# A graph-attention kernel: the message product reads its weights from PSUM, VectorE copies them, and the logits have three PSUM banks for four

## The reference

```python
xl = (x @ W_l).reshape(n, H, C)          # n = 6250, H = 4 heads, C = 64
xr = (x @ W_r).reshape(n, H, C)
feat = xl[src] + xr[dst]
feat = jnp.where(feat >= 0, feat, NEG_SLOPE * feat)
logits = jnp.einsum('ehc,hc->eh', feat, att)
seg_max = jax.ops.segment_max(logits, dst, num_segments=n)
ex = jnp.exp(logits - seg_max[dst])
seg_sum = jax.ops.segment_sum(ex, dst, num_segments=n)
alpha = ex / (seg_sum[dst] + 1e-16)
msg = alpha[:, :, None] * xl[src]
out = jax.ops.segment_sum(msg, dst, num_segments=n)
```

## Time and profile before

| | |
|---|---|
| time, median of 3 runs | 2216.73 us (2213.54 to 2217.0) |
| span of the profiled execution, first to last instruction | 2209.5 us |
| what the median has beside that span | 7.2 us |
| busy share: TensorE, VectorE, GpSimd, ScalarE | 85%, 68%, 57%, 55% |
| attention gathers, first to last start | 172.33 to 1398.80 us |
| memory traffic over the span | 191 GB/s |

### The profile page before, as it was taken

One profiled execution on the slowest core, in us unless ns is written; L12 is line 12 of the kernel. 1 busy time (PEld: TensorE's weight loads), 2 busy tenths in 40 slices (PEclk: granted clock), 3 DMA queues, 4 the chain that ended last, 5 costly groups with the idle time before them and its releaser, 6 DMA issues. The chain is left out here.

```text
span 2209.5 us, 43411 instructions
## 1 busy us (share of the span) xinstructions
PE 1888.2 (85%) x9692; PEld 1605.4 (73%) x9693; DVE 1508.1 (68%) x3609; ACT 1205.5 (55%) x2834; POOL 1268.0 (57%) x1207
## 2 busy tenths in 40 slices
PE   2995899998999999989899998878958449999996
PEld 1774677777777777777777777678847348888885
DVE  5985799998999899999889989875467501111110
ACT  2553576766766666666667666656456213232221
POOL 3336777777777777777777777200016723444444
PEclk9997999999999999999999999989955579999998
DMA  7677777777777777777777777267014655666664
GB/s 210 230 249 240 231 229 230 224 230 225 225 226 221 232 226 227 225 224 230 225 225 226 229 226 226 63 200 243 1 48 157 168 155 138 141 144 144 141 147 63
DMA packets 256712, 422.34 MB, mean 191 GB/s; under 512 B 45801, under 2 KB 128088, under 8 KB 256652
## 3 DMA queue, kind: packets, MB, share of 16 engines
q1 hardware_dynamic: 154608, 223.36, 32.2%
q0 software_dynamic: 65408, 153.31, 27.4%
q10 hardware_dynamic: 36636, 45.00, 6.4%
HBM read 358.65 MB, written 62.86 MB: 191 GB/s over the span
## 5 line engine op out<-in xcount | busy, mean ns | idle before, releaser
L822 POOL DMA_INDIRECT ring<-xl_rows,a_idx x928 | 944.9, 1018 | 290.0 <-issue 234.3
L1139 PE MATMUL a_f_ps<-a_xr_w,a_hot_n 128*128 128x256 f32 x1856 | 529.6, 367 | 134.4 <-DMA ring<-xl_rows,a_idx 104.2
L1141 PE MATMUL a_f_ps<-ring,ident 128*128 128x256 f32 x1856 | 558.9, 383 | 0.0
L1139 PEld LDWEIGHTS a_f_ps<-a_xr_w,a_hot_n 128*128 128x128 f32 x1856 | 336.3, 191 | 263.8 <-issue 150.0
L1152 PE MATMUL a_o_ps<-ring,a_hot_e 128*128 128x264 f32 x1856 | 491.6, 390 | 1.3 <-DVE ring L1024 1.0
L1152 PEld LDWEIGHTS a_o_ps<-ring,a_hot_e 128*128 128x128 f32 x1856 | 350.3, 192 | 57.6 <-issue 2.5
L1006 DVE SCALAR_TENSOR_TENSOR a_pos<-a_f_ps,att_cols 128x512 f32<-128x512 f32 x464 | 315.8, 681 | 60.9 <-PE a_f_ps L1141 59.5
L1016 DVE TENSOR_REDUCE a_lg<-a_pos 128x8 f32<-128x512 f32 x464 | 316.4, 682 | 26.1 <-PE a_sm_ps L1162 25.4
L1024 DVE TENSOR_TENSOR ring<-ring (+1 forms) x464 | 316.8, 683 | 1.7 <-ACT ring L931 1.7
L2031 POOL DMA_INDIRECT out_dram<-ring,x_idx x106 | 165.9, 1565 | 259.3 <-issue 126.9
L896 ACT ACTIVATE a_far_e<-iota_row,a_near_rel 128x128 f32<-128x128 f32 x928 | 294.8, 388 | 1.3
(11 more groups left out here) (349 smaller groups left out, 2164.7 us busy)
## 6 DMA issues: line engine op xcount, KB each, us to landing
a_xr_w<-xr_rows SPq DMA_DIRECT2D x464, 256.0 KB
a_rel_bc<-rel_rows ACTq DMA_DIRECT2D x116, 256.0 KB
x_w<-in_L_ffn_W_dram SPq DMA_DIRECT2D x57, 512.0 KB, 4.3
ring<-xl_rows,a_idx POOLq DMA_INDIRECT x928
xr_rows<-xr_parts SPq DMA_DIRECT2D x50, 256.0 KB, 2.1
ring<-disp_rows SPq DMA_DIRECT2D x49, 257.0 KB, 2.7
xl_rows<-xl_sb SPq DMA_DIRECT2D x50, 132.0 KB, 1.8
j_xl<-xl_rows SPq DMA_DIRECT2D x25, 264.0 KB, 2.9
```

Of the source, the lines that this page charges most:

```text
L822: nc.gpsimd.indirect_dma_start(xl_e[:, p * T + 2 * h + u, :], None, k.xl_rows, bass.IndirectOffsetOnAxis(ap=idx[:, p, 2 * h + u:2 * h + u ...
L1139: nc.tensor.matmul(f_ps[:, h % FS, u, :], hot_n[:, j % 2, 2 * g + u, :], xr_w[:, h % XR, a, :].bitcast(F32R), start=(a == 0), stop=False)
L1141: last = nc.tensor.matmul(in_heads(f_ps[:, h % FS, u, :]), k.ident[:, :], heads_of(xl_e[:, p * T + 2 * h + u, :])[:, :, 0:C], start=False, ...
```

## The change

The product takes its weights straight from `turn_ps`, which gets a PSUM bank of its own. For that bank the logits give up one of their four, and take turns in the order in which the sums do (`slot`, `freed_by`: places 0, 1, 2 in turn, with place 1 for unit 15). The copy of weights and maxima into the ring, which the sums still need, moves from ScalarE to VectorE, just ahead of the product for unit 0. TensorE's turn of the weights now waits until VectorE has made all messages of the chunk before (`msg_ready`), since they read the bank; its sums wait for the copy (`exs_ready`); its turn of the logits no longer does.

```diff
-    FS = 4
-    o_slot = lambda h: 1 if h == NU - 1 else h % 3
-    o_freed_by = lambda h: h - (4, 2, 4)[h] if h < 3 else h - 2 if h == NU - 1 else h - 3
+    slot = lambda h: 1 if h == NU - 1 else h % 3
+    freed_by = lambda h: h - (4, 2, 4)[h] if h < 3 else h - 2 if h == NU - 1 else h - 3
...
-        f_ps = pb("a_f_ps", [P, FS, 2, D])
+        f_ps = pb("a_f_ps", [P, 3, 2, D])
...
-        lgr_ps, turn_ps, fade_ps = sm_ps[:, 0:P], sm_ps[:, P:3 * P], sm_ps[:, 3 * P:3 * P + H + 1]
+        lgr_ps, fade_ps = sm_ps[:, 0:P], sm_ps[:, P:P + H + 1]
+        turn_ps = pb("a_turn_ps", [P, 512])
+        exs_of = turn_ps[:, 0:P].rearrange("p (h t) -> p t h", t=T)
...
-                def weights(c, half):
-                    act.wait_ge(turned, c)
-                    act.sem_inc(k.taken, 1)
-                    out = half.rearrange("p t (h w) -> p t h w", w=XC)[:, :, :, C:XC]
-                    nc.scalar.copy(out.rearrange("p t h a -> p a h t"),
-                                   turn_ps.rearrange("p (a h t) -> p a h t", a=2, t=T)).then_inc(exs_ready, 1)
...
-                        if soft_in and j == 3:
-                            weights(c, ring)
...
+                def weights(cc, half):
+                    dve.wait_ge(turned, cc + 1)
+                    out = half.rearrange("p t (h w) -> p t h w", w=XC)[:, :, :, C:XC]
+                    nc.vector.tensor_copy(out.rearrange("p t h a -> p a h t"),
+                                          turn_ps[:, 0:2 * P].rearrange("p (a h t) -> p a h t", a=2, t=T)).then_inc(exs_ready, 1)
...
                     if hh == 0:
-                        dve.wait_ge(exs_ready, cc + 1)
+                        weights(cc, half)
...
-                    nc.vector.tensor_tensor(at[:, :, :, 0:C], at[:, :, :, 0:C], at[:, :, :, C:C + 1].to_broadcast([P, 2, H, C]),
+                    nc.vector.tensor_tensor(at[:, :, :, 0:C], at[:, :, :, 0:C],
+                                            exs_of[:, 2 * hh:2 * hh + 2, :, None].to_broadcast([P, 2, H, C]),
...
-                    wait_past(pe, settled, c * NU + (h - FS + 1))
+                    wait_past(pe, settled, c * NU + (freed_by(h) + 1))
...
+                    if hh == 0:
+                        pe.wait_ge(exs_ready, cc + 1)
                     pe.wait_ge(msg_ready, cc * NU + (hh + 1))
...
                 def turn_logits(cc):
                     pe.wait_ge(lg_ready, (cc + 1) * NU)
-                    wait_past(pe, exs_ready, cc)
...
                 def turn_weights(cc):
                     pe.wait_ge(masks, 1)
+                    wait_past(pe, msg_ready, cc * NU)
```

More of the change, by code:

```diff
@@ L1005, in settle @@
                     dve.wait_ge(f_done, c * NU + (h + 1))
-                    nc.vector.scalar_tensor_tensor(pos[:, h % 2], f_ps[:, h % FS], 0.0, att, ALU.max,
+                    nc.vector.scalar_tensor_tensor(pos[:, h % 2], f_ps[:, slot(h)], 0.0, att, ALU.max,
                                                    ALU.mult).then_inc(settled, 1)
@@ L1035, in add_up @@
                     at = k.acc[:, bass.ds(block, 1), :].rearrange("p o w -> p (o w)")
-                    nc.vector.tensor_tensor(at, o_ps[:, o_slot(hh), 0:XW], at, ALU.add).then_inc(added, 1)
+                    nc.vector.tensor_tensor(at, o_ps[:, slot(hh), 0:XW], at, ALU.add).then_inc(added, 1)
                 def softmax(cc, part, block=None):
@@ L1135, in logits_of @@
                     pe.wait_ge(landed[h % LANDS], c * (32 * NU // LANDS) + (h // LANDS + 1) * 32)
-                    wait_past(pe, settled, c * NU + (h - FS + 1))
+                    wait_past(pe, settled, c * NU + (freed_by(h) + 1))
                     for u in range(2):
                         for a in range(PARTS):
-                            nc.tensor.matmul(f_ps[:, h % FS, u, :], hot_n[:, j % 2, 2 * g + u, :], xr_w[:, h % XR, a, :].bitcast(F32R),
+                            nc.tensor.matmul(f_ps[:, slot(h), u, :], hot_n[:, j % 2, 2 * g + u, :], xr_w[:, h % XR, a, :].bitcast(F32R),
                                              start=(a == 0), stop=False)
-                        last = nc.tensor.matmul(in_heads(f_ps[:, h % FS, u, :]), k.ident[:, :],
+                        last = nc.tensor.matmul(in_heads(f_ps[:, slot(h), u, :]), k.ident[:, :],
                                                 heads_of(xl_e[:, p * T + 2 * h + u, :])[:, :, 0:C], start=False, stop=True)
@@ L1148, in sums_of @@
                         pe.wait_ge(hot_e_ready, cc * QUADS + (j + 1))
+                    if hh == 0:
+                        pe.wait_ge(exs_ready, cc + 1)
                     pe.wait_ge(msg_ready, cc * NU + (hh + 1))
-                    wait_past(pe, added, cc * NU + (o_freed_by(hh) + 1))
+                    wait_past(pe, added, cc * NU + (freed_by(hh) + 1))
                     for u in range(2):
-                        last = nc.tensor.matmul(o_ps[:, o_slot(hh), 0:XW], hot_e[:, j % 2, 2 * g + u, :],
+                        last = nc.tensor.matmul(o_ps[:, slot(hh), 0:XW], hot_e[:, j % 2, 2 * g + u, :],
                                                 xl_e[:, pp * T + 2 * hh + u, :], start=(u == 0), stop=(u == 1))
```

## The result

The changed kernel took 2220.73 us (median of 8 runs, 2217.27 to 2222.53), the kernel before, beside it, 2214.15 us. The ratio is 1.0028, with a 95% interval of 1.0019 to 1.0037: slower by 6.6 us, where 2166 us was forecast. The profiled execution spans 2218.5 us, 9.0 more than before.

A forecast was written before the change was run, and what follows sets the result against it. GpSimd's gathers, some held by message products, were taken to bound the attention loop. 2209.5 - 56 (hold) + 1.5 (tail) + 4 (backlog) = 2159.0 us span; with 7.2 for the median, 2166 us, range 2156 to 2196.

The forecast's parts named there:

- What bounds the kernel, and the hold: Attention loop: GpSimd's gathers set the pace; message products with two SBUF inputs hold some; removing the hold gives -56 us.
- The removed parts and the banks: ScalarE's copy gone: 0 taken; three logits banks: 0, at worst 0.5 us a chunk; removed `exs_ready` wait: 0.
- VectorE's copy: VectorE's added copy of 256 elements from PSUM: 0.34 us a chunk, at worst 0.63, at best nothing.
- TensorE's new wait, `msg_ready`, ahead of turn_weights: After logits(6): TensorE waits 2 us a chunk; VectorE's addition(6) stalls 0.7 to 0.8, at most 2.2.
- the prediction's own sum: VectorE's chunk: 38.5 + 0.34 copy + 0.75 stall = 39.6 us, 0.6 below GpSimd's new pace of 40.2.
- Rival 1: VectorE becomes the pace through a 2.2 us stall or 0.63 us copy: 2180 to 2210 us; chance 0.18.
- gaps of GpSimd over 0.30 us: Sign in the profile after, between GpSimd's gathers, that would speak for rival 1.
- Rival 2: The hold stays with one SBUF input, or isn't the pace: 2217 us, at most 2219; chance 0.07.
- Rival 3: Message product with PSUM second input takes longer, over 0.85 us: slower, 2287 us at 1.0 us a product; chance 0.09.
- VectorE busy above 95%: Expected sign in the profile after: VectorE's busy share in the attention stage, 92% before.
- The end of the stage: After the last gather, the wait delays the turn by about 1.4 us: +1.5, at most 2.5; backlog charged separately, 4 us.
- The 7.2 us between span and median: Median of runs lies 7.2 us above the profiled span, taken as untouched work around it and added to 2159.0.

The follow-up runs named there:

- the later turn: Changed kernel with TensorE turning the weights after its logits of unit 7 instead of unit 6; 2156.80 us (ratio 0.9741).
- the first experiment: Kernel before with three banks and the product's second input an idle PSUM bank of ones, ScalarE's copy and all waits kept; 2156.66 us beside 2214.92 (0.9741).

## Why the prediction was wrong

**What bounds the kernel, and the hold.** Right. GpSimd was the pace, a product with two SBUF inputs held its gathers, and taking the hold away, with three banks, gave 58.3 us by the medians and 55.8 by the spans (2209.5 less 2153.7), where -56 stood in the sum. A detail was off: the four long gathers outside a product carry 1.2 us (they take 1424, 1366, 1133 and 1128 ns), not 0.7. The product's duration was forecast at 683 ns and is 679.

**The removed parts and the banks.** Right: three banks alone change nothing that can be measured. ScalarE's copy was put at 0; no run takes it away by itself, and the later turn, which has it removed, is level with the first experiment, which keeps it (2156.80 and 2156.66 us).

**VectorE's copy.** It takes 0.48 us of VectorE (837.02 to 837.50) where 0.34 was forecast, inside the bounds given. Without the hold it costs nothing that can be seen, by the same two times. With the hold in place it came to 6 us, by more held gathers, a path that the prediction didn't have.

**The step that failed: "TensorE's new wait, `msg_ready`, ahead of turn_weights".** Its place, what is queued behind it and who waits for that were right. Two sizes in it were not. The wait was put at 2 us a chunk and is 3.5; with the clock kept up, 2.6 us pass there. And the turn and sums(6) behind it were taken at the durations of the earlier trace rows, 0.62 and 1.05 us, which are those of a TensorE that hasn't stood still. After the wait they take 1.18 and 1.97 in the chunk shown. So VectorE's stall, forecast at 0.7 to 0.8 us with 2.2 as the bound, is 2.46 in the chunk shown and up to 2.9. With it VectorE's chunk is 39.6 - 0.75 + 2.5 = 41.4 us by the prediction's own sum, over GpSimd's 40.2. The logits of unit 7 came 5.0 us after the product (832.34 plus 0.68, to 837.97), where 3.1 stood. VectorE, stalled itself, still took them without a wait:

```profile
838.68 0.68 DVE L998 SCALAR_TENSOR_TENSOR a_pos<-a_f_ps,att_cols 128x512 f32<-128x512 f32 x1
```

The chunk came to (1398.6 - 172.4) / 927 x 32 = 42.3 us, just what it was before. The sum of VectorE's own time gives 41.4, as this isn't one engine's need but a loop through two. From the turn to the turned logits of the next chunk, TensorE works without a stop at 2.22 us a unit, slower than VectorE at 2.13, and VectorE follows it. From there, VectorE's softmax parts and units 0 to 5 decide when TensorE may turn again. The slow clock stretches the first half, by 2.2 us a chunk on average. Over the 27 chunks with the wait that is about 60 us.

The trace of before had shown it. In the earlier trace rows the same turn follows a wait of 2.77 us, and its first pair of matmuls takes 0.56 us, twice the 0.28 of the earlier trace rows. The prediction used that row for its start time and not for its duration. The windows of the kernel before say the same, there and once in the middle of the loop, after a wait of 2.29 us for gathered rows that ended at 721.34:

```profile
721.30:725.00 3.70, 3.66 (x12) 3.01 (x13) 0.69 (x1) 1.09 (x3) 2.79 (x4) 0.57 0.51 135
...
1416.50:1420.00 3.50, 3.46 (x11) 3.02 (x12) 1.34 (x3) 1.92 (x6) 0.00 (x0) 0.50 0.00 0
```

Not every wait of that length does it: after one of 2.04 us that ended at 1356.85, the next 3.7 us had a clock of 1.00.

The Trainium skill states in "TensorE: Matmul & The Clock Gate", section "What's actually happening", that TensorE falls to 1.2 GHz when it has stood idle; the traces here agree, 0.53 after the wait of 3.44 us and 0.50 after that of 2.77. The prediction didn't weigh this rule.

**The rivals.** Rival 1, VectorE as the pace for a stall of 2.2 us in place of 0.75, named the right place, and its sign came: gaps of GpSimd over 0.30 us. It stopped at 2208, as it didn't have the clock. Of its conditions the stall held, 2.46 us for 2.2. Rival 2, that the hold stays, gave at most 2219 us, close to what was measured, by chance: its cause isn't there, as the mean gather fell to 0.961 us. Rival 3, the one on the slower side, blamed the product, which takes 679 ns. VectorE busy above 95% was forecast as well; it is 180.42 of 200 us, as it waits in the loop.

**The end of the stage.** The new wait puts off the last turn by 1.4 us, as forecast. The turned logits there came 6.4 us later than before (1413.77 for 1407.38) and the turn 7.8 us later (1424.30 for 1416.54), though the last gather started at the same time. These 6.4 us are the backlog of an engine pair that no longer keeps up with GpSimd, where the prediction had charged 4.

**The 7.2 us between span and median.** They were called work around the span. The runs' own times lie 1.8 to 1.9 us over their spans (2220.39 us for a span of 2218.5); the rest was the spread between executions. It plays no part in the miss.

## What to carry to other kernels

A wait added to TensorE's queue can cost more than its length: price the instructions behind it at the lower clock, take their durations from a place in the trace where TensorE had stood still, and check the sum of the loop with those. If the wait can't go, give TensorE its own next work first (here one unit later, 64 us) or, failing that, matmuls that nobody reads. And where GpSimd issues indirect DMAs, compare the mean of a gather with its median: a gap means that something holds them.

## What the runs showed of the hardware

- An indirect gather that starts early in a VectorE tensor_tensor with both inputs in SBUF is held. In the kernel before, 200 gathers start during a product, 154 of them in its first 0.41 us. Of these 153 last over 1.1 us, up to 1.49 for 0.96, and they all end 1.50 to 1.52 us after the product began. Those that start 0.56 us or more into it take 0.96. With one input in PSUM (the changed kernel) 181 gathers start in the first 0.41 us and none is held; the mean is 0.958 to 0.961 us over 928 gathers in five kernels. VectorE's own time is the same in both cases, 677 to 684 ns.
- TensorE came back at 0.53 of its clock after 3.44 us of standing still, and worked at 0.98 again in the stretch from 836.7 us on; one chunk later the 5.8 us after the wait (875.5 to 881.3 us) had 0.51. Matmuls whose result nobody reads kept it at 1.00.
- The same place in the queue cost the whole 60 us of the removed hold when TensorE stood idle in it (2220.73 us), and some 3 us (2160.20 us, for 2156.80 with the later turn) when it ran matmuls there. These two times come from different sets of runs, and the intervals of their ratios overlap.
